# A one-layer token tower on one core: the residual of the MLP seeded into PSUM, biases added by TensorE, and the small products of the recurrence reordered between the engines

## The reference

```python
h = take(quantised table, x)                       # 64 x 128 x 256
h = h + block(layernorm(h))
h = h + ffn_int8(layernorm(h))                     # one scale from max |layernorm(h)| of all rows
# block(x):
x = x + mixer(rms(x)); return x + fc2(gelu(fc1(rms(x)) + b1)) + b2
# mixer: in_proj -> zgate (512), u (512), B (16), C (16), dt (8); a causal 4-tap convolution and silu on u, B, C
Bc = Bc * rsqrt(sum(Bc*Bc) + 1e-6); Cc likewise; dt = softplus(dt + dt_bias)
# per token t, per head, 64 x 16 states:
z = (z + d * (Bu - A * y)) / (1 + d*d*A);  y = y + d * z;  out = y . C_t
# then (out + D_skip * u) * silu(zgate), out_proj and its bias
```

## Time and profile before

| quantity | value |
|---|---|
| profiled execution | 1418.98 us, its span 1417.2 us |
| median of three runs | 1417.96 us |
| busy TensorE, VectorE | 1148.7 us (81%), 1181.0 us (83%) |
| busy ScalarE, GpSimd | 755.9 us (53%), 802.1 us (57%) |
| first part | 0 to about 179 us |
| turns of the pipeline | about 188 to 1360 us |
| mean granted TensorE clock | 0.954 of full speed |

### The profile page before, as it was taken

The page is one execution under the profiler, slowest core; times in us unless marked ns, Lnnn a source line. Parts: engine busy times, 40 slices in busy tenths (PEclk is TensorE's granted clock), DMA queues, the critical chain, the costliest instruction groups (busy, mean ns, idle before and its releaser), DMA issues. The chain is left out here.

```text
span 1417.2 us, 25541 instructions
## 1 busy us (share of the span) xinstructions
PE 1148.7 (81%) x7199; PEld 761.4 (54%) x7206; DVE 1181.0 (83%) x2167; ACT 755.9 (53%) x1108; POOL 802.1 (57%) x2246
## 2 busy tenths in 40 slices
PE   0595033499898989898989999898989898989766
PEld 0353021357575757475756566565657575757444
DVE  4899948788888988888888888889898988888277
ACT  4667343464646473737383738373646555551247
POOL 7870013485767667585858575857575858570100
PEclk9999996599999999999999999999999999999889
DMA  9999500000001010101010000000000000000015
GB/s 363 408 408 423 221 17 17 18 19 17 24 10 33 0 33 0 33 2 31 6 28 11 23 16 18 17 17 17 17 17 17 17 17 19 17 17 1 0 45 193
DMA packets 62069, 92.22 MB, mean 65 GB/s; under 512 B 9101, under 2 KB 55010, under 8 KB 57554
## 3 DMA queue, kind: packets, MB, share of 16 engines
q1 hardware_dynamic: 58386, 82.10, 16.3%
q0 software_dynamic: 3072, 8.39, 1.5%
q10 hardware_dynamic: 576, 1.31, 0.3%
HBM read 81.29 MB, written 10.49 MB: 65 GB/s over the span
## 5 line engine op out<-in xcount | busy, mean ns | idle before, releaser
L748 POOL TENSOR_TENSOR stp<-Gs,X 128x32 f32<-128x32 f32 x984 | 280.0, 285 | 270.1 <-ACT X L723 171.2
L750 POOL TENSOR_TENSOR Gs<-Gs,stp 128x32 f32<-128x32 f32 x984 | 279.5, 284 | 76.9
L605 PE MATMUL bank<-xT,w_in 128*128 128x512 f32 x512 | 242.3, 613 | 49.1 <-DVE uT L861 49.1
L1059 PE MATMUL bank<-mT,w_fc 128*128 128x512 f32 x512 | 244.0, 616 | 2.0 <-ACT mT L1047 2.0
L1078 PE MATMUL bank<-w_fc,gl 128*128 128x256 f32 x1024 | 243.1, 381 | 0.0
L1078 PEld LDWEIGHTS bank<-w_fc,gl 128*128 128x128 f32 x1024 | 191.0, 190 | 59.3 <-issue 32.0
L605 PEld LDWEIGHTS bank<-xT,w_in 128*128 128x128 f32 x512 | 93.8, 193 | 158.5 <-issue 87.8
L847 ACT ACTIVATE uT<-bank,cols 128x512 f32<-128x512 f32 x64 | 47.8, 775 | 211.3 <-DVE sz L973 163.5
L1059 PEld LDWEIGHTS bank<-mT,w_fc 128*128 128x128 f32 x512 | 99.5, 200 | 99.6 <-issue 94.8
L861 DVE SCALAR_TENSOR_TENSOR uT<-bank,cols,uT 128x500 f32<-128x500 f32 (+1 forms) x192 | 134.7, 738 | 2.3
L340 DVE TENSOR_TENSOR peak<-ring,peak 128x1536 f32<-128x1536 f32 (+2 forms) x67 | 115.3, 1722 | 19.8 <-ACT ring L243 18.4
(11 more groups left out here) (173 smaller groups left out, 1957.2 us busy)
## 6 DMA issues: line engine op xcount, KB each, us to landing
ring<-in_table SPq DMA_DIRECT2D x32, 1536.0 KB, 20.8
d_rep<-d_rows SPq DMA_DIRECT2D x128, 64.0 KB, 2.7
out<-res SPq DMA_DIRECT2D x16, 512.0 KB, 2.9
b_rep<-bc_rows SPq DMA_DIRECT2D x128, 32.0 KB, 1.8
c_rep<-bc_rows SPq DMA_DIRECT2D x128, 32.0 KB, 1.8
w_fc<-in_w_fc SPq DMA_DIRECT2D x2, 1024.0 KB, 8.7
w_in<-in_w_in ACTq DMA_DIRECT2D x1, 1088.0 KB, 5.1
h<-in_table,ids POOLq DMA_INDIRECT x64, 9.5
```

Source lines behind the costliest of these rows:

```text
L605: last = pe.matmul(dst, w_in[:, k, c0:c1], xT[:, k, :], start=(k == 0), stop=(k == KD - 1))
L748: pool.tensor_tensor(stp[:], Gs[:, t, ::-1, :], X2[:, t, :, :], ALU.mult).then_inc(rec.sem, 1)
L750: pool.tensor_tensor(Gs[:, t + 1, :, :], Gs[:, t, :, :], stp[:], ALU.add).then_inc(rec.sem, 1)
L1059: last = pe.matmul(pj[n % 4][:, :], w_fc1[:, k, n * P:(n + 1) * P], mT[:, k, :], start=(k == 0), stop=(k == KD - 1))
```

## The change

The diff, cut to its core. Semaphore counts that only follow are left out; a line in round brackets or behind # tells what stands there.

```diff
-        out_b = sb("out_b", [P, D])
-        fc2_b = sb("fc2_b", [P, D])
+        bias3 = sb("bias3", [P, 2, 2 * D], BF16)
+        pick = sb("pick", [P, P], BF16)
...
-        LATE_WEIGHTS = ((w_fc1, "w_fc1"), (w_out, "w_out"), (w_fc2, "w_fc2"), (out_b, "out_b"), (fc2_b, "fc2_b"))
+        LATE_WEIGHTS = ((w_fc1, "w_fc1"), (w_out, "w_out"), (w_fc2, "w_fc2"))
...
-            HOT_FROM = 8
+            HOT_FROM = 4
+                def tier_top(t0, t1):      # the fold of L369 to L378, for tiers t0 to t1 alone
...
+                    if n == upper - 1:     # after the tiles of tiers 1, 2 and the rest tile, now fifth
+                        tier_top(0, 2)
+                tier_top(2, 3)             # after the last tile, which comes as two halves
```

The biases are split into three bf16 parts, on partitions 0, 64 and 96, and one bf16 product with `pick` (ones on these three rows) adds them:

```diff
+        def dve_split_biases(dve):         # five DVE operations on up to 128x1024, in turn 0
+                pe.matmul(sbk[n][:, :], pick[:], bias3[:, OUT_B, :], start=True, stop=False, skip_group_check=True)
                 (before the out products of each half, in pe_out)
+                for i in range(2):
+                    pe.matmul(sbk[i][:, :], pick[:], bias3[:, FC2_B, :], start=False, stop=False,
                 (before fc2 product 0, in pe_fc2, behind a wait for seeded)
+        def act_seed(act, g):              # xl (the residual) goes to the two banks of fc2
+            act.wait_ge(xmT_ready.sem, xmT_ready.at(g))
+            act.wait_ge(x2_ready.sem, x2_ready.at(g))
+            for n in range(2):
+                act.activation(sbk[n][:, :].rearrange("p (j c) -> p j c", j=2), xl[:, 2 * n:2 * n + 2, :], ACT.Copy) \
-        def pool_residual(pool, g):        # both additions go
-        def dve_layer_norm(dve, g):
+        def act_layer_norm(act, g):        # four ACT Identity with bias off1, scale rs1
-        def dve_rms_rows(dve, g):
+        def act_norm_rows(act, g):         # four ACT Identity with bias lnst[7], scale lnst[6]
-        def dve_rms(dve, g):
+        def pool_rms(pool, g):
+            pool.wait_ge(ssq_ready.sem, ssq_ready.at(g))
+            pool.tensor_tensor(ssq[:, 1, :], ssq[:, 0, :], eps6[:], ALU.add).then_inc(rsq.sem, 1)
+            pool.wait_ge(rsq.sem, rsq.at(g, 1))
+            pool.tensor_tensor(ssq[:, 2, :], ssq[:, 1, :], half[:], ALU.pow).then_inc(rsq.sem, 1)
```

`pool_norm_factors` gets two operations more, `pool_rstd3` three. `dve_x2` becomes one addition of 128x512 per half. `dve_max3`'s four subtractions become `act_x3`, one turn later (a fourth stage, and a turn GROUPS + 2). `dve_keys` does the key products and the C products first and only then waits for the squares. The orders of a turn:

```diff
         act_turn
                 if first:
                     act_small_in(act, g)
+                if third:
+                    act_seed(act, m)
                 if first:
+                    act_small_silu(act, g)
                     act_small_dt(act, g)           # now with preload_act_table_set("natural_log_exp_and_others")
+                if first:
+                    act_small_norm(act, g)
+                    act_small_rsqrt(act, g)
                 for n in range(FT):
                     (gelu n)
-                    if second and n == 1:
+                    if second and n == 0:
                         act_squares(act, p)
-                    (small_silu after 2, rep after 4 and 5, small_norm after 6)
+                    (rep after 2 and 3)
+                (after utok: act_layer_norm(p), act_x3(g - 3), u_tap0, act_norm_rows(g + 1), silu_u 0 to 2, ...)
         pe_turn
-                    if first and n == 6:
+                    if first and n == 1:
                         pe_ss(pe, g)
         dve_turn
+                (dve_bk(p) after conv_small; after the gates: conv_u 0, 1, conv_u 2, x2 0, conv_u 3, x2 1,
+                 dve_bc, dve_max3(g - 3), stats3, mean3; in turn 0: dve_bc, dve_split_biases, first_steps)
         pool_turn
-                if third:
-                    pool_residual(pool, m)
                 if first and second:
                     pool_recurrence(pool, g, range(0, CL // 2))
                 if nxt:
                     pool_norm_factors(pool, g + 1)
+                if first and third:
+                    pool_recurrence(pool, g, range(CL // 2, RMS_STEP))      # RMS_STEP = 52
+                    pool_rms(pool, p)
+                    pool_recurrence(pool, g, range(RMS_STEP, CL))
+                elif first:
+                    pool_recurrence(pool, g, range(CL // 2 if second else DVE_STEPS, CL))
+                if second and not (first and third):
+                    pool_rms(pool, p)
                 if third:
                     pool_rstd3(pool, m)
```

More of the change, by code:

```diff
@@ L365, in _ @@
                         dve.tensor_copy(ident_b[:], ident[:])
[L366 to L379, removed]
+                tier_top(2, 3)
                 dve.wait_ge(maxT, 1)
                 dve.tensor_reduce(tmaxr[:, 0:1], bank[2][0:4, 0:P], AX.X, ALU.max).then_inc(max_step, 1)
[L382 removed]
+                dve.wait_ge(max_step, 2)
                 dve.tensor_scalar(diag[:], ident[0:4, 0:4], tmaxr[:, 0:1], None, ALU.mult).then_inc(max_step, 1)
@@ L1195, in act_turn, with turn @@
         def act_turn(act):
-            def turn(g, first, second, third, nxt):
+            def turn(g, first, second, third, fourth, nxt):
                 p, m = g - 1, g - 2
@@ L1237, in turn @@
                 if first:
-                    act_silu_u(act, g, (2,))
+                    act_silu_u(act, g, (3,))
                 if second:
                     act_sum_squares(act, p, 1)
-                if first:
-                    act_silu_u(act, g, (3,))
+            act_norm_rows(act, 0)
             turns(act, turn)
         def dve_turn(dve):
-            def turn(g, first, second, third, nxt):
+            def turn(g, first, second, third, fourth, nxt):
                 p, m = g - 1, g - 2
@@ L1251, in turn @@
                     dve_conv_small(dve, g)
+                if second:
+                    for hg in range(HG):
+                        dve_bk(dve, p, hg)
                 if first:
@@ L1275, in turn @@
                     dve_gate(dve, p, (2, 3))
+                if first:
+                    dve_conv_u(dve, g, (0, 1))
+                    dve_conv_u(dve, g, (2,))
+                if second:
+                    dve_x2(dve, p, 0)
+                if first:
+                    dve_conv_u(dve, g, (3,))
+                if second:
+                    dve_x2(dve, p, 1)
+                if first and second:
+                    dve_bc(dve, g)
+                if fourth:
+                    dve_max3(dve, g - 3)
                 if third:
@@ L1316, in turn @@
                     pool_norm_factors(pool, g + 1)
+                if first and third:
[6 more added lines that the diff above has]
+                    pool_rms(pool, p)
                 if third:
                     pool_rstd3(pool, m)
-                if first:
-                    pool_recurrence(pool, g, range(CL // 2 if second else DVE_STEPS, CL))
             pool_norm_factors(pool, 0)
@@ L1326, in _, with turn @@
             def _(sp):
-                def turn(g, first, second, third, nxt):
+                sp.dma_start(utok[:, 0:2, :], a["bias"].rearrange("p (i c) -> p i c", i=2)).then_inc(bias_in, 16)
+                def turn(g, first, second, third, fourth, nxt):
                     if first:
```

264 lines of the change are left out of this document (138 added, 126 removed).

## The result

The changed kernel takes **1379.06 us** (median of 4 runs, 1378.4 to 1381.66), the kernel before 1417.76 in the same runs: ratio **0.9727, 95% interval 0.971 to 0.9744**. One execution of experiment 2 (3047 us) and one of experiment 8 (1502 us) were slow ones; they are in the medians given there (1373.84 and 1419.38 without them), not in the ratios. The profiled execution took 1378.95 us, its span is 1377.1.

The account below looks back on a forecast made before the run. A turn was TensorE's work plus four short waits; after the change GpSimd's ring would decide. Terms summed to -23.1 us, mainly -24.2 from thirteen turns against +9.7 in turn 1, giving 1395 us, range 1381 to 1412.

Parts of the forecast that it names:

- GpSimd's ring: Chain through GpSimd's recurrence, RMS factor and small product back to the first step: 66.3 us a turn, said to decide.
- X to R: GpSimd's stretch from the recurrence's first step (X) to the RMS factor ready (R): 42.9 us.
- S to X: From the end of the small product (S) to the recurrence's first step (X): 18.1 us, before 19.8.
- TensorE's ring: TensorE's own work and short waits over one turn: 64.1 to 65.4 us, the shorter of two rings.
- turn 1: Turn without a third stage, its RMS factor waits for all 64 recurrence steps: +9.7 us.
- dd: VectorE operation between softplus and the replicated d: some 0.3 us long instead of 2.46.
- TensorE decides: Rival: GpSimd reaches step 52 two us sooner, TensorE sets the turn; 1382 us, chance 0.12.
- VectorE's small operations: Rival: they block GpSimd on the way to step 52, 0.5 to 1.2 us a turn; 1408 us, chance 0.15.
- slower: Rival: VectorE's new order blocks GpSimd steps from norm factors to step 52; 1433 us, chance 0.13.
- No gain: Rival: TensorE's wait ahead of the normed MLP rows stays, 68.2 us a turn; 1418 us, chance 0.05.
- costs of nothing: Edits counted as free because covered by waits, among them key products moved ahead of squares, queries later needed by scores.
- The rule on table loads: Skill's added drain of about 1380 ns per table switch, left out; with it the sum some 18 us lower.

Follow-up runs that it names:

- experiment 2: Kernel after with the RMS factor taken behind step 44 of the recurrence, not 52: 1374.19 us, ratio 0.9683, a turn 64.31 us.
- experiment 8: Kernel after with key and C products put back behind the squares' sum, as in the kernel before: 1419.45 us, ratio 0.999.
- Experiment 1: Kernel before with two filling matmuls in TensorE's 2.42 us wait ahead of the MLP's row transposes: 1406.71 us, ratio 0.9914.
- experiment 3: Kernel after with the RMS factor taken behind step 60 of the recurrence: 1467.6 us, ratio 1.0348.
- experiment 5: Kernel after without the second preload of the softplus's table (a 1.28 us load): 1379.66 us, ratio 0.971.
- experiment 4: Kernel after with the RMS factor taken behind step 52 in turn 1 too, instead of all 64 steps: 1370.67 us, ratio 0.9665.
- experiment 6: Kernel after without the second table preload and with the RMS factor behind step 48: 1357.05 us, ratio 0.9557, a turn 63.28 us.
- experiment 10: Kernel after with the RMS factor taken behind step 54 of the recurrence: 1405.89 us, ratio 0.9908.

## Why the prediction was right in kind and wrong in size

**The step that failed** is in GpSimd's ring: "the small product ended at 719.32: 5.3 us, and the same operations follow here". The same operations follow, but not at the same clock. In the kernel after, the factor is ready at 702.74 + 1.02 = 703.76 and the small product ends at 707.17 + 1.08 = 708.25: **4.5 us**. The 5.3 held a small product of 1.93 us, run behind a 2.42 us wait at a granted clock of 0.65. The forecast said itself that this wait would shrink, to "1 to 2 us", and yet carried over a duration that belonged to the longer wait. Both clock levels of the same 32 matmuls stood in the rows: 1.93 in the earlier trace rows, 1.08 in the earlier trace rows. Experiment 1 shows the term alone, 0.86 us of a turn; the rest of the stretch, from the factor to the start of the small product, is 3.4 us in both kernels.

The second, smaller error is X to R: 42.9 forecast, 768.80 - 726.32 = 42.5 measured; the first 32 steps took 22.8 us, not 23.5, with fewer collisions with VectorE than in the earlier trace rows (norm factors and twenty steps took 18.35, forecast 18.0; the pair 1.3, forecast 1.4). S to X was right (18.1 forecast, 726.32 - 708.25 = 18.07). Ring: 42.48 + 4.49 + 18.07 = 65.04. The forecast's ring is 66.3, but its gain per turn counts with 66.4, a slip worth 1.3 us in all. So of 13 x 1.36 = 17.7 us the clock is 11, X to R 5.5 and the slip 1.3; 1.5 goes the other way, as the thirteen old turns took 68.14 us on average and not 68.26. That leaves the 16 of the table. The range was too narrow for the same reason: its low end was built on TensorE's ring as a rival, not on a ring of GpSimd that might be shorter itself.

**Right:** which ring decides (experiments 2, 3 and 5: shortening it gives 0.7, lengthening it costs in full, taking TensorE's own 0.76 us wait away gives the whole nothing that can be told from noise); turn 1, whose cause experiment 4 confirms; the waits ahead of z 2 and z 3; dd; the gathers' wait until 113 us; a bias product, 758.86 - 758.64 = 0.22 us. The wait ahead of the first MLP transposes was 7.63 us, forecast some 10.

**In range by luck:** TensorE's ring, 64.1 to 65.4, measured 64.3. It holds the same 1.9 us for the small product. By the forecast's own sum it should have been 65.3 with the second load paid, where experiment 2 has 64.31, and 64.1 without it, where experiment 6 has 63.28: both times about 0.85 to 1.0 too long.

**Rivals.** "TensorE decides", 1382, came nearest in time and is refuted in cause: GpSimd's pair has no idle time ahead of it. "VectorE's small operations" and "slower" needed more collisions than before; there were fewer. "No gain", 1418, is the time of experiment 8, by another mechanism: through one edit that the forecast had put among its costs of nothing. I had asked there whether the queries would be late, and not whether the recurrence's first step, which waits for VectorE's reads of the states, would overtake them: in the kernel after, that read ends at 722.57 + 1.03 = 723.6 and the step stands at 726.3. The cover was 2.7 us, less than the 4.1 us of the products that were moved out of its way.

**Smaller terms.** Up to turn 1 the change gave 2.9 us, not 5.6. The closing folds went from 6.7 to 2.8 us, as forecast within 0.4, but did not start earlier (168.21, before 168.20), where 0.7 was forecast. From them to the first small product 2.4 us were lost (forecast 1.9), and turn 0 gave 1.45 (52.27, before 53.72), not 2.5. In the timeline of the kernel after they are:

```profile
168.21 0.96 DVE L352 TENSOR_TENSOR peak<-peak 128x768 f32<-128x768 f32 x1
...
170.59 0.42 DVE L364 TENSOR_REDUCE tmax<-colmax 128x1 f32<-128x256 f32 x1
```

The last MLP's rows wait 1.40 us for GpSimd where they waited 6.20 for the Newton chain, -4.8 against -4.7 forecast:

```profile
1277.26 1.70 ACT L1058 ACTIVATE xr<-xl,ssq 128x256 f32<-128x256 f32 x4 [1.40 <-POOL ssq L1049]
```

The other 2.6 us of the end, spread over the last turn and the output, were not taken apart.

**The rule on table loads** that the forecast set aside stays aside. The Trainium skill, page "ScalarE: Activation LUTs", section "What ACT_TABLE_LOAD costs", adds a drain of about 1380 ns to the 1283 ns of a load for a switch to a different set. By it the forecast's sum would have been some 18 us lower, about 1377, and so near the measured 1379 for a cause that the trace does not show. Experiment 5 takes a load away and 1.28 us go; that load fetched the set that was active already, so it doesn't test a switch. At the switch ahead of the exponential the load begins at 711.03 in the kernel after, 0.02 behind the end of the activation before it, and the next activation at 712.33, 0.02 behind the load's end.

## What to carry to other kernels

A duration read behind a long wait of TensorE belongs to that wait: where the change shortens it, take the same operation from a turn in which the clock was up, and keep the other value for the range. When two rings lie within a microsecond, an edit to the wrong one is worth nothing and the same edit is worth its full price once the other is gone, as the table load was (experiments 5 and 6), so compute the second ring before judging an edit by its run. For each edit costed at nothing ask what waits for it on every engine, not only what it was moved past: the order of four products was worth 40 us in the kernel after and 0 in the kernel before.

## What the runs showed of the hardware

A wait of 0.54 us (kernel after, 705.72) or 1.09 us (experiment 5, 640.91) left TensorE's granted clock at 1.00. Behind 2.42 us (kernel before, 715.94) the transposes still ran at the full level and the small product at the lower one; behind 2.79 us (experiment 8) the granted clock was 0.54 over both, behind 5.49 us (experiment 3) 0.50. Behind 1.72 to 2.11 us (experiment 10) the small product was sometimes fast and sometimes slow. The lower level took the small product from 1.08 to 1.94 us and the transposes from 1.09 to 1.97, and redundant matmuls in the wait were a net gain of 12 us (experiment 1).

A table load is paid again, 1.28 us, when the set it names is already active (713.25 in the kernel after; experiment 5 does without it).

An operation of the recurrence on GpSimd, 128x32, mostly took 0.25 us; the two that ran beside VectorE's product of the queries (L870, 128x512, both inputs in SBUF, from 731.90 in the kernel after) took 1.07 and 0.88.
